# A message-passing kernel: counts kept in bf16 and turned in runs of eight, bias rows made in one pass, the matmul engine's loop written out, and slot masks moved from GpSimd to VectorE

## The reference

```
# layer 0: relational message passing, 8 edge kinds, 4 basis matrices
m    = sum over b of  w_comp[kind, b] * (x[src] @ V[b]) * edge_weight
agg  = segment_sum(m, dst)
h    = relu(agg + x @ loop_w + bias)
x1   = layernorm(x + layernorm(h @ ffn_w.T + ffn_b + x) * ln_g + ln_b)
# layer 1: two attention convolutions over the same edges, 2 heads of 64
alpha = (q[dst] . k[src]) / 8 ;  softmax over the edges of each dst
out   = segment_sum(v[src] * a, dst) + x @ Ws + bs
```

## Time and profile before

| | |
|---|---|
| median of 3 runs | 2248.89 us (2246.86 to 2251.12) |
| profiled execution | 2249.5 us, span 2247.5 us, mean clock 0.981 |
| message stage, to the first instruction of `conv` | 54.8 to 1220.9 us of the span |
| PE busy | 2104.2 us, 94% of the span |
| DVE, ACT, POOL busy | 1590.5, 1291.7, 821.2 us |

### The profile page before, as it was taken

How to read it: one execution, slowest core, us unless ns; L and a number is a source line. 1 busy time by engine, 2 the same in 40 slices (tenths; PEclk the granted TensorE clock), 3 DMA queues, 4 the chain that set the end, 5 groups by cost and what they waited for, 6 DMA issues and landing times. The chain is left out here.

```text
span 2247.5 us, 55086 instructions
## 1 busy us (share of the span) xinstructions
PE 2104.2 (94%) x19640; PEld 1707.9 (76%) x19640; DVE 1590.5 (71%) x4061; ACT 1291.7 (57%) x2303; POOL 821.2 (37%) x1091
## 2 busy tenths in 40 slices
PE   1299999999999999999997999999999999999998
PEld 1288888898888888888985677777776677777776
DVE  1458887888888888878873666666664666666765
ACT  1156666665666666666663555556564455565555
POOL 0766776777677667767710000000000000000000
PEclk9599999999999999999998999999999999999999
DMA  4001111111111111111112222222221122222220
GB/s 122 14 31 45 42 46 51 44 45 52 47 38 46 51 48 41 46 51 44 43 40 100 87 78 72 80 85 85 85 85 48 71 94 92 92 92 92 92 92 7
DMA packets 52538, 141.57 MB, mean 63 GB/s; under 512 B 9261, under 2 KB 43755, under 8 KB 45855
## 3 DMA queue, kind: packets, MB, share of 16 engines
q1 hardware_dynamic: 49804, 129.55, 16.3%
q0 software_dynamic: 2576, 9.68, 1.5%
HBM read 93.95 MB, written 45.27 MB: 62 GB/s over the span
## 5 line engine op out<-in xcount | busy, mean ns | idle before, releaser
L778 PE MATMUL ps<-matrixT,x_rows 125*128 125x256 f32 (+1 forms) x2500 | 582.7, 384 | 2.9 <-ACT aggT L864 2.1
L778 PEld LDWEIGHTS ps<-matrixT,x_rows 125*128 125x128 f32 x2500 | 461.4, 191 | 70.9 <-issue 3.3
L845 ACT COPY matrixT<-ps 125x500 f32<-125x500 f32 (+2 forms) x800 | 395.8, 583 | 201.5 <-PE ps L766 197.3
L1468 ACT COPY weightsT_l<-ps 125x500 f32<-125x500 f32 (+1 forms) x450 | 233.8, 542 | 369.2 <-PE ps L1389 369.2
L766 PE MATMUL ps<-high_weights,low_onehot 64*125 64x125 f32 x6300 | 403.8, 279 | 23.2 <-issue 11.3
L1546 DVE CUSTOM_DVE_ANT_0 scores_l<-ps,bias_rows_l 125x500 f32<-125x500 f32 (+1 forms) x700 | 396.8, 619 | 35.3 <-issue 33.7
L766 PEld LDWEIGHTS ps<-high_weights,low_onehot 64*125 64x125 f32 x6300 | 366.2, 189 | 54.0 <-issue 37.2
L1389 PEld LDWEIGHTS ps<-eye,scores_l 125*125 125x125 f32 x2500 | 301.1, 189 | 115.6 <-issue 97.2
L1389 PE MATMUL ps<-eye,scores_l 125*125 125x125 f32 x2500 | 364.2, 286 | 4.8 <-ACT scores_l L1450 3.4
L1554 DVE COPY weightsT_l<-ps 125x500 f32<-125x500 f32 (+1 forms) x250 | 150.0, 600 | 267.3 <-PE ps L1389 264.9
L1450 ACT ACTIVATE scores_l<-scores_l,neg_max_l 125x1500 f32<-125x1500 f32 x200 | 320.9, 1605 | 20.5 <-DVE neg_max_l L1583 20.4
(11 more groups left out here) (154 smaller groups left out, 1864.5 us busy)
## 6 DMA issues: line engine op xcount, KB each, us to landing
bias_rows_l<-bias SPq DMA_DIRECT2D x50, 1562.5 KB, 6.7
bias<-bias SPq DMA_DIRECT2D x150, 250.0 KB
edges<-rec POOLq DMA_DIRECT2D x1, 2014.2 KB, 11.8
x_rows<-in_x SPq DMA_DIRECT2D x1, 1562.5 KB
bias<-bias SPq DMA_DIRECT2D x25, 62.5 KB
x<-x_rows SPq DMA_DIRECT2D x25, 62.5 KB
x_rows_l<-x SPq DMA_DIRECT2D x25, 62.5 KB
out<-rows_l SPq DMA_DIRECT2D x25, 62.5 KB
```

What stands on the lines that cost most here:

```text
L778: last = nc.tensor.matmul(psG[:, BASES * SPLIT * side:BASES * (SPLIT * side + SIDE[side])], x[:, h, :], MT[side][:, 0:SIDE[side], BASES * ...
L845: last = nc.scalar.copy(MT[side][:, at:at + 2 * c - 1:2, 0:COLS], psP[bank][0:R, :].rearrange("p (i c) -> p i c", c=128)[:, 0:c, 0:COLS])
L1468: nc.scalar.copy(PT[i % 8][:, 0:cw[c]], psT[i % 2][0:R, 0:cw[c]]).then_inc(z["pa_ok"], 1)
```

## The change

- `CT` becomes bf16; the counts are turned by bf16 transposes against a bf16 identity, into the same bank seen as eight bf16 planes. A tile's 25 planes go in runs of 8, 8, 8 and 1 (in periods k = 1, 3, 5, 6) where there were seven groups of up to 4. The bank is given back by ACT's logarithm (`ln_ok`), since DVE no longer reads it.
- A bias row is one instruction, min(1e28 * ln, ln), on 1000 columns; the two instructions on 500 columns go. The stores are of 500 KB.
- `slot_kinds` is new: DVE masks the slots, writes the digit planes, and makes the weighted kinds with eight instructions of 64 columns. It stands at the end of DVE's step for tile t-1. POOL's `coefs` keeps the four coefficient rounds. The buffers `node_p` and `held2` go.
- `turn_codes` and ACT's two copies after it move from k = 4 to k = 5.
- PE's whole message program is written out (no loop); the other engines keep theirs. On ACT, in k = 7, the copy of x stands behind `counts_out`.

```diff
--- before.py
+++ after.py
 PIECES = 4
+RUN = 8
+RUN_AT = {1: 0, 3: 1, 5: 2, 6: 3}
+FAR = 1.0e28
 PARTS = (0, 6, 12, 18, T)
 AFTER, LEAD = 5, 7
-COEF_STEPS = 19
+COEF_STEPS = 15
 OWN = 512.0
...
         MT = [sb(f"matrixT{i}", [R, SPLIT, 128], F32) for i in range(2)]
-        CT = sb("countsT", [R, T, R], F32)
+        CT = sb("countsT", [R, T, R], BF16)
+        eye16 = sb("eye16", [128, 128], BF16)
         aggT = sb("aggT", [D, BASES, R], F32)
         xt = sb("xT_tile", [128, R], F32)
-        lns = [sb(f"ln{i}", [R, CW], F32) for i in range(2)]
-        bias = [sb(f"bias{i}", [128, CW], F32) for i in range(2)]
+        lns = [sb(f"ln{i}", [R, RUN * R], F32) for i in range(2)]
+        bias = [sb(f"bias{i}", [128, RUN * R], F32) for i in range(2)]
         tiny = sb("tiny", [128, 1], F32)
         spare = sb("spare", [128, 1], F32)
         hrow = sb("m_h_rows", [R, D], F32)
...
                 then = Steps(pool, gps, s * COEF_STEPS)
-                e = ell[par].rearrange("p (s c) -> p c s", c=FIELDS)
                 to = codes[par]
-                then(nc.gpsimd.tensor_copy(node_p[:, :], ids[:, bass.ds(s, 1)]))
-                pool.wait_ge(ell_in[par], (half(s, par) + 1) * 16)
-                hold(2, s)
-                then(nc.gpsimd.tensor_scalar(off[:, :], e[:, 4, :], node_p[:, :], OWN, ALU.is_equal, ALU.mult))
                 if not is_int(s) or s >= 2:
                     pool.wait_ge(codes_ps, s - 1)
-                nc.gpsimd.tensor_tensor(to[:, 0, :], e[:, 0, :], off[:, :], ALU.add)
-                nc.gpsimd.tensor_copy(to[:, 1, :], e[:, 1, :])
-                for r in range(RELS):
-                    last = nc.gpsimd.tensor_scalar(kinds[:, r, :], e[:, 2, :], float(r), None, ALU.is_equal)
-                then(last)
-                then(nc.gpsimd.tensor_tensor(kinds[:, :, :], kinds[:, :, :], e[:, 3:4, :].to_broadcast([128, RELS, SLOTS]), ALU.mult))
+                pool.wait_ge(kinds_ok, s + 1)
                 for b in range(BASES):
...
             def find_slots(s, par):
+                if not is_int(s) or s >= 2:
+                    pool.wait_ge(kinds_ok, s - 1)
                 pool.wait_ge(slot_ok, s + 1)
...
-            def store(u, par, j):
-                n, at = u * CH + j, (par + j) % 2
-                sp.wait_ge(bias_ok, n + 1)
-                sp.dma_start(m["bias"][bass.ds(u, 1), :, CW * j:CW * j + cw[j]].rearrange("a p n -> (a p) n"),
-                             bias[at][:, 0:cw[j]]).then_inc(out_ok[at], 16)
+            def store(u, i):
+                at, (g, k) = i % 2, runs[i]
+                sp.wait_ge(bias_ok, u * PIECES + i + 1)
+                sp.dma_start(m["bias"][bass.ds(u, 1), :, g * R:(g + k) * R].rearrange("a p n -> (a p) n"),
+                             bias[at][:, 0:k * R]).then_inc(out_ok[at], 16)
             def step(t, par):
-                if inside(t - 5):
-                    store(t - 5, 1 - par, CH - 1)
                 if inside(t - 4):
-                    for j in range(CH - 1):
-                        store(t - 4, par, j)
+                    for i in range(PIECES):
+                        store(t - 4, i)
                 if inside(t - 5):
             pipeline_loop(sp, step, AFTER, LEAD)
-            sp.wait_ge(out_ok[0], 16 * ((T * CH + 1) // 2))
-            sp.wait_ge(out_ok[1], 16 * (T * CH // 2))
+            for at in range(2):
+                sp.wait_ge(out_ok[at], 16 * (T * PIECES // 2))
             sp.wait_ge(kept[0], 16 * ((T + 1) // 2))
...
             V.tensor_scalar_add(own_low[:, :], iota[:, 0:R], OWN)
+            V.tensor_copy(eye16[:, :], eye[:, :])
             V.memset(tiny[:, :], 1.0e-37).then_inc(const, 1)
...
                                        ALU.add).then_inc(slot_ok, 1)
+            def slot_kinds(s, par):
+                then = Steps(v, s3, s)
+                e = ell[par].rearrange("p (s c) -> p c s", c=FIELDS)
+                v.wait_ge(ell_in[par], (half(s, par) + 1) * 16)
+                then(V.tensor_scalar(off[:, :], e[:, 4, :], node[par][:, :], OWN, ALU.is_equal, ALU.mult))
+                if not is_int(s) or s >= 1:
+                    v.wait_ge(codes_ok, s)
+                for r in range(RELS):
+                    V.scalar_tensor_tensor(kinds[:, r, :], e[:, 2, :], float(r), e[:, 3, :], ALU.is_equal, ALU.mult)
+                if not is_int(s) or s >= 2:
+                    v.wait_ge(codes_ps, s - 1)
+                V.tensor_tensor(codes[par][:, 0, :], e[:, 0, :], off[:, :], ALU.add)
+                V.tensor_copy(codes[par][:, 1, :], e[:, 1, :]).then_inc(kinds_ok, 1)
...
-            def bias_row(u, par, j):
-                n, at = u * CH + j, (par + j) % 2
-                row = bias[at][0:R, 0:cw[j]]
+            def bias_row(u, i):
+                n, at = u * PIECES + i, i % 2
+                cols = runs[i][1] * R
                 v.wait_ge(ln_ok, n + 1)
                 if not is_int(u) or n >= 2:
-                    v.wait_ge(out_ok[at], (n - at) // 2 * 16)
-                V.tensor_scalar(row, psT[0:R, 0:cw[j]], 0.0, NEG, ALU.is_equal, ALU.mult).then_inc(masked, 1)
-                v.wait_ge(masked, n + 1)
-                V.tensor_tensor(row, row, lns[at][:, 0:cw[j]], ALU.add).then_inc(bias_ok, 1)
+                    v.wait_ge(out_ok[at], (u * (PIECES // 2) + i // 2) * 16)
+                ln = lns[at][:, 0:cols]
+                V.scalar_tensor_tensor(bias[at][0:R, 0:cols], ln, FAR, ln, ALU.mult, ALU.min).then_inc(bias_ok, 1)
...
                     if k == 0 and inside(z):
-                        bias_row(z, 1 - par, CH - 1)
                         second(z, 1 - par)
...
                         search_row(t - 1, 1 - par)
-                    if k >= 2 and inside(u):
-                        bias_row(u, par, k - 2)
+                    if k - 1 in RUN_AT and inside(u):
+                        bias_row(u, RUN_AT[k - 1])
                     if k == 5 and inside(u):
...
                         build_hot(w + 1, par, k + AHEAD - PERIODS)
+                    if k == PERIODS - 1 and inside(t - 1):
+                        slot_kinds(t - 1, 1 - par)
             pipeline_loop(v, step, AFTER, LEAD)
...
-            def turn_counts(u, j):
-                n = u * CH + j
-                if j % 2 == 0:
-                    pe.wait_ge(ctA_ok, u * PIECES + (j // 2 + 1))
-                    pe.wait_ge(ctB_ok, u * PIECES + (j // 2 + 1))
-                if not is_int(u) or n >= 1:
-                    pe.wait_ge(masked, n)
-                for i in range(cw[j] // R):
-                    last = nc.tensor.transpose(psT[0:R, R * i:R * (i + 1)], CT[:, 4 * j + i, :], eye[0:R, 0:R])
+            def turn_counts(u, i):
+                n, (g, k) = u * PIECES + i, runs[i]
+                pe.wait_ge(ctA_ok, n + 1)
+                pe.wait_ge(ctB_ok, n + 1)
+                if n >= 1:
+                    pe.wait_ge(ln_ok, n)
+                for h in range(g, g + k):
+                    last = nc.tensor.transpose(psC[0:R, h - g, 0:R], CT[:, h, :], eye16[0:R, 0:R])
                 last.then_inc(c_ps, 1)
...
                         sums(w, 0, k - 4)
-                    if k >= 1 and inside(u):
-                        turn_counts(u, k - 1)
+                    if k in RUN_AT and inside(u):
+                        turn_counts(u, RUN_AT[k])
                     if k == 4 and inside(u):
...
                         nc.tensor.transpose(psM[:, 128:128 + R], hrow[:, :], eye[0:R, 0:R]).then_inc(h_ps, 1)
-                    if k == 4 and inside(w + 1):
+                    if k == 5 and inside(w + 1):
                         turn_codes(w + 1, par)
...
                         nc.tensor.transpose(psM[:, 384:384 + R], xnew[1 - par][:, :], eye[0:R, 0:R]).then_inc(x_ps, 1)
-            pipeline_loop(pe, step, AFTER, LEAD)
+            pipeline_loop(pe, step, AFTER, T)
...
                 if side == 0 and (not is_int(s) or s >= 1):
-                    act.wait_ge(c_ps, s * CH - CH + min(2 * piece + 2, CH))
+                    act.wait_ge(c_ps, s * PIECES - PIECES + piece + 1)
                 act.wait_ge(evac_ok, s * PERIODS + PERIODS // 2 * (side + 1))
...
-            def logs(u, par, j):
-                n, at = u * CH + j, (par + j) % 2
+            def logs(u, i):
+                n, at, k = u * PIECES + i, i % 2, runs[i][1]
                 act.wait_ge(c_ps, n + 1)
                     act.wait_ge(bias_ok, n - 1)
-                nc.scalar.activation(lns[at][:, 0:cw[j]], psT[0:R, 0:cw[j]], ACT.Ln, bias=tiny[0:R, :]).then_inc(ln_ok, 1)
+                nc.scalar.activation(lns[at][:, 0:k * R].rearrange("p (h n) -> p h n", n=R), psC[0:R, 0:k, 0:R], ACT.Ln,
+                                     bias=tiny[0:R, :]).then_inc(ln_ok, 1)
...
                         counts_out(u, 1, 3)
-                    if k == 7 and inside(z):
-                        act.wait_ge(x_ps, z + 1)
-                    if k >= 1 and inside(u):
-                        logs(u, par, k - 1)
```

(19 more changed lines are left out.)

12 lines of the change are left out of this document (6 added, 6 removed).

## The result

The changed kernel took 2190.16 us (median, 2189.22 to 2191.13), the kernel before beside it 2248.39 us: a ratio of 0.974, 95% interval 0.9723 to 0.9757.

What follows compares the result with a forecast made beforehand. PE was taken to set the message stage's pace, DVE next. Savings of 11.8 + 3.4 + 1.5 + 2.5 + 3.4 + 1.5 = 24.1 us gave 2225 us against the median of 2248.9, range 2196 to 2239.

Steps and rivals of the forecast that it cites:

- the transposes do shrink: Rival, 28%: in the message stage one bf16 transpose every 0.057 us, saving 32.5 us in place of 2.5; 2195 us.
- bf16 transposes, 2.5 us: PE's 625 count transposes in the message stage: rhythm set by the weight load, 0.105 us, saving 2.5 us.
- PE written out, 11.8 us: PE's message loop: eight jumps back stall it about 1.4 us each; straight code saves 11.8 us.
- Codes, 3.4 us: PE's waits for POOL before turn_codes: codes ready some 6 us earlier and wanted a period later, saving 3.4 us.
- these three: ACT, DVE and POOL in the steady state, waiting 1.1 us at a time, 6.6 and 10.1 us a step.
- Start, 3.4 us: First tile: POOL's 6.45 us before the coefficient rounds becomes 3.0 us on DVE, saving 3.4 us.
- End of stage, 1.5 us: Last tile of the message stage, where turn_counts and first wait: 1.5 us saved, between 0 and 3.
- DVE's work: DVE per tile in the message stage: net +0.4 us, hidden by a margin of 6.6 us.
- aggT, 1.5 us: ACT's period 7 loses its short logarithm, aggT comes earlier, most of its 2.4 us of waits goes: 1.5 us.
- Runs of eight: Seven transpose groups a tile become four: 0 saved, as moving between groups showed no cost.
- The slower rival: Rival, 7%: a short stream hides no load, 0.152 us a transpose, 26.9 us lost on them; 2254 us.
- stalls elsewhere: Rival, 13%: PE's fetches, other engines' jumps or a late DVE keep the 11.8 us; 2237 us.

## Why the prediction was wrong

The signs were right, one size was far off, and one reading of waits was wrong. The rival "the transposes do shrink" came near with its 2195 us, in part by luck: it had the rhythm, but neither it nor the forecast knew of the ring, and the parts that open it were in the change for other reasons. Term by term:

- **bf16 transposes, 2.5 us: the step that failed.** It read "If the stream shrinks to 0.052 us and the load stays, the rhythm is that of the load". The load did not stay: 0.80 ns a column was taken as a property of the width, and it is one of the type as well (137 to 138 ns at 125 columns in bf16, 189 in f32). The rhythm is 0.057 us, the lower bound that the first rival stood on; 625 x 0.052 = 32.5 us, and 28.8 measured with turn_codes later. The row of 128 columns in the earlier trace rows showed that the rate was not fixed, and was set aside because the planes stay 125 wide. The Trainium skill ("TensorE: Matmul & The Clock Gate", Weight-path perf modes) has the fast load need 128 columns and a type other than f32. Here bf16 was enough at 125 columns, and in f32 128 columns were enough in a transpose (141 to 143 ns), though not in an ordinary product (191 ns). The Trainium skill's 81 ns between matmuls of 128 columns (same page, Back-to-back issue gap) is above the 57 ns of 125 columns here.
- **PE written out, 11.8 us: right.** 12 alone. Within the kernel after it is 7.4, as a jump costs less there (4.5 us for the eight).
- **Codes, 3.4 us: the waits go, but the reading failed.** "Work that goes from these three is worth nothing in the steady state" took POOL's wait of 10.1 us a step for a margin. POOL's wait is part of a ring that is closed in every other step, and such a wait says nothing of how late POOL may be. Had the transposes been sized rightly, the sum would still have needed this: bf16 alone is worth 4 us, 23 to 29 with one cure of the ring. Five parts of the change shorten or open the ring (later turn_codes, masks off POOL, one-pass rows, no jump in it, runs of eight); the last three together are enough within it, by 0.23 us, and the first two are its margin. Without the runs of eight the ring would just close, by an estimate from their 0.65 us in it and 0.2 us a step on PE; it was not run.
- **Start, 3.4 us: 4.4.** DVE does the eight kinds in 1.55 us, 0.18 each from start to start in place of 0.27.
- **End of stage, 1.5 us: 5.3.** The one-pass rows alone shorten it by 4.5. A bias row of 1000 columns lasts 1.20 us there (1.28 on the average of the stage), not 1.92, and DVE has one instruction between the last logarithm and `first`. For the same reason DVE's work did not grow by 0.4 us a tile but fell, from 662 to 624 of 785 us.
- **aggT, 1.5 us:** its waits are gone from 265 to 1050 us; they are no more than a part of the step's 1.53.
- **Runs of eight, 0: up to 0.2 us a step**, 5 us (42.08 against 41.87), and their 0.65 us in the ring.

Together: of the 48.2 us of the budget 11.8 are the jumps, and 36.4 are left for the steps, 1.46 us each if there are 25; a step with all its work is 1.53 shorter, and the first ones, which have no counts yet, less. With 4.4, 5.3 and 1.2 in `conv` it is 59.1, the difference of the spans. The slower rival (load and stream add up) is ruled out by 0.057 us; stalls elsewhere did not come: PE is busy 785 of 785 us.

## What to carry to other kernels

When one engine is busy 98% and still waits a little for another, look for a ring before you call the other's waits a margin: follow the late buffer back through each engine's program order, and if the chain returns to the engine after one step, compare its length with the step, in a turn where the engine does wait. If they are alike, a saving needs both bounds moved, and one part of a change tried alone will mislead. When two mean steps agree, look at the single steps and at the granted clock before you call them the same. The element type changed both the load and the stream of these short matmuls; measure one group in the new type before costing it by the old one.

## What the runs showed of the hardware

- A bf16 load of 125 columns lasts 137 to 138 ns where f32 takes 189, and an f32 transpose's load of 128 columns 141: three columns more, 48 ns less. The f32 loads of 128 columns in ordinary products last 191. Loads and matmuls of 125 columns in bf16 follow each other every 57 ns.
- An f32 product is two matmuls in the trace and a bf16 one is one; a transpose is one in both (625 records either way).
- 20 transposes ahead of a loop of PE, none of them on the path, made the kernel 11 us slower; each iteration then had a second stall, 8.8 us in all.
- With bf16 alone the granted clock fell to the 1.2 GHz level four times in the loop (0.53 over 339.0 to 342.6 us), each time right behind a wait of 1.8 us; each cost 1.6 us, and other waits as long had no such fall behind them.
- A DVE instruction of three operands on 64 f32 columns took 0.27 us from start to end and 0.18 us in a row of eight; on 1000 columns 1.20 us at the stage's end and 1.28 on the average.
